# One GIN graph layer on one core: register loads of 32, copies moved to VectorE, 22 gathered rows a group on both queues, a reordered end

## What is computed

```
h   = relu(layernorm(x))
agg = segment_sum(h[src], dst)            # 200000 rows gathered
t   = relu(batchnorm(((1 + eps) h + agg) @ W1 + b1))     # 512 wide
y   = t @ W2 + b2 + h
out = x + relu(batchnorm(y))
```

## Time and profile before

| | |
|---|---|
| median of 3 runs | 3151.29 us (3143.07 to 3159.94) |
| the profiled execution | 3149.71 us |
| its span (first to last instruction) | 3147.9 us |
| around the span | 1.8 us |
| granted TensorE clock, mean | 0.72 |
| busy: PE / PEld / DVE / ACT / POOL | 46 / 29 / 20 / 15 / 45 % |

### The profile page before, as it was taken

The page is one execution under the profiler, slowest core; times in us unless marked ns, Lnnn a source line. Parts: engine busy times, 40 slices in busy tenths (PEclk is TensorE's granted clock), DMA queues, the critical chain, the costliest instruction groups (busy, mean ns, idle before and its releaser), DMA issues.

```text
span 3147.9 us, 31339 instructions
## 1 busy us (share of the span) xinstructions
PE 1454.9 (46%) x4883; PEld 918.7 (29%) x4883; DVE 632.1 (20%) x1628; ACT 472.7 (15%) x979; POOL 1431.3 (45%) x1518
## 2 busy tenths in 40 slices
PE   2443444444434434443352453344444253444999
PEld 2222222333222222232231232222223132322546
DVE  6454531111101101111011011011011010111346
ACT  4553530000000000000000000000000000000445
POOL 5645455555444453454344544544544454553000
PEclk7766677776776776776676766767766666767999
DMA  5544432332222222222222322222322222233646
GB/s 162 169 142 145 135 111 87 93 100 79 86 87 71 87 87 78 85 87 80 75 73 84 96 71 80 83 82 87 93 74 80 76 90 80 79 92 120 235 161 255
DMA packets 129207, 325.72 MB, mean 103 GB/s; under 512 B 35641, under 2 KB 61594, under 8 KB 122862
## 3 DMA queue, kind: packets, MB, share of 16 engines
q0 software_dynamic: 72384, 197.75, 21.3%
q1 hardware_dynamic: 43946, 99.32, 8.8%
q10 hardware_dynamic: 12676, 26.68, 2.6%
HBM read 271.56 MB, written 52.05 MB: 103 GB/s over the span
## 4 chain that ended last, share of the span: by engine, by line
SPq 47%; issue 28%; PE 8%; ACTq 2%; another core or an unknown queue 0%; DVE 0%; ACT 0%; DVEq 0%; DMA 0%
SPq L482 38%; SPq L477 8%; PE ps L1345 5%; ACTq L1102 2%; PE ps L1359 1%; SPq L446 1%; PE ps L1301 0%; PE ps L1228 0%; PE ps L1263 0%; SPq L467 0%; SPq L451 0%; ACTq L1098 0%; DVE aggT L789 0%; DVE st L632 0%
## 5 line engine op out<-in xcount | busy, mean ns | idle before, releaser
L606 POOL DMA_INDIRECT arena<-h_rows,arena x1272 | 1205.4, 948 | 1262.9 <-PE ps L1228 755.7
L1228 PE MATMUL ps<-arena 128*96 128x256 f32 x3016 | 940.1, 478 | 754.1 <-issue 217.9
L1228 PEld LDWEIGHTS ps<-arena 128*96 128x96 f32 x3016 | 624.2, 212 | 1047.0 <-issue 619.9
L1254 PE MATMUL ps<-ident,arena 128*128 128x128 f32 x196 | 55.6, 381 | 668.7 <-ACT aggT L1055 357.5
L606 POOL DMA_INDIRECT arena<-in_x,arena x220 | 208.5, 948 | 197.2 <-PE ps L1228 112.6
L828 DVE BATCH_NORM_STATS2 arena<-arena 128x6 f32<-128x512 f32 x92 | 63.7, 693 | 1080.4 <-ACT arena L1071 788.9
L1254 PEld LDWEIGHTS ps<-ident,arena 128*128 128x128 f32 x196 | 26.8, 183 | 717.9 <-issue 685.3
L789 DVE TENSOR_TENSOR aggT<-aggT,ps 128x192 f32 x196 | 69.4, 354 | 739.6 <-PE ps L1238 357.4
L1263 PE MATMUL ps<-arena 128*128 128x512 f32 (+3 forms) x412 | 209.9, 639 | 1.3 <-DVE arena L820 1.1
L1062 ACT COPY arena<-ps 96x256 f32<-96x256 f32 x196 | 71.8, 367 | 899.1 <-issue 688.6
L1055 ACT COPY aggT<-ps 128x256 f32<-128x256 f32 x98 | 36.0, 369 | 1039.6 <-issue 1025.6
(11 more groups left out here) (94 smaller groups left out, 532.8 us busy)
## 6 DMA issues: line engine op xcount, KB each, us to landing
rl_odd<-h_rows SPq DMA_DIRECT2D x3456, 1.0 KB
W2s<-h_rows ACTq DMA_DIRECT2D x3072, 1.0 KB
t_T<-arena SPq DMA_DIRECT2D x24, 1024.0 KB, 3.8
arena<-t_T SPq DMA_DIRECT2D x24, 1024.0 KB, 4.8
arena<-h_rows,arena POOLq DMA_INDIRECT x1272
arena<-in_x SPq DMA_DIRECT2D x27, 512.0 KB, 5.6
h_rows<-arena ACTq DMA_DIRECT2D x24, 512.0 KB
out<-arena SPq DMA_DIRECT2D x23, 512.0 KB
```

What stands on the lines that cost most here:

```text
L606: nc.gpsimd.indirect_dma_start(out=rows[slot(g)][:, k, :], out_offset=None, in_=(x if g < H_FROM else h_dram)[:, :], in_offset=bass.Indire ...
L1228: last = T.matmul(win_ps[g % 2], sel[:, g % 2, k, :], rows_of(g, k), start=k == 0, stop=k == n - 1)
L1254: last = T.transpose(hT[:, f, 0:n], h[0:n, f * P:(f + 1) * P], ident[0:n, 0:n])
```

## The change

Seven edits:

1. SP and ScalarE load 32 row addresses at a time instead of 16 (AT_ONCE); each register is freed once its row is issued.
2. ScalarE's share rises from 20 to 22 rows a group (ACT_EIGHTHS = 11). It then fetches 27 tiles instead of 24, and GpSimd 1505 instead of 1508. SP's share stays at 22 rows a group, counted in eighths.
3. From group 31 (COPIES_FROM) on the copies `keep_window`, `keep_hT` and `t_and_b1` of the main loop are VectorE's. The last ones, after the loop, stay ScalarE's.
4. Inverse, shift and normalisation of group 0 stand ahead of the flag.
5. SP stores the last full chunk of t after its wait for all windows, not before it.
6. y is added, measured and signalled for each half f by itself, on TensorE and on VectorE; the residual addition and the store of the last output chunk are cut into two halves.
7. `keep_warm` around the last groups: 8, 3, 10 and 26 multiplications become 4, 1, 6 and 12.

```diff
-SP_QUARTERS = 11
-ACT_QUARTERS = 5
+SP_EIGHTHS = 22
+ACT_EIGHTHS = 11
+COPIES_FROM = H_FROM + 1
+AT_ONCE = 32
...
             def load_rows(j, m):
...
-                regs = [sp.alloc_register(f"row{j}_{m}_{k}") for k in range(PIECE)]
-                sp.reg_load(regs, sp_at[j % 2][0:1, m * PIECE:(m + 1) * PIECE])
+                if m * PIECE % AT_ONCE == 0:
+                    regs = [sp.alloc_register(f"row{j}_{m}_{k}") for k in range(AT_ONCE)]
+                    sp.reg_load(regs, sp_at[j % 2][0:1, m * PIECE:m * PIECE + AT_ONCE])
+                    row_regs.extend(regs)
                 for k in range(PIECE):
                     e = m * PIECE + k
-                    at = sp.snap(regs[k], donate=True, min_val=0, max_val=(N - 1) * ROW_BYTES)
+                    reg = row_regs.pop(0)
+                    at = sp.snap(reg, donate=True, min_val=0, max_val=(N - 1) * ROW_BYTES)
...
-                for reg in regs:
                     sp.free_register(reg)
...
+            sp.wait_ge(s_add, NG)
             store_t(NQF - 1)
-            sp.wait_ge(s_add, NG)
             for q in range(X_FIRST):
                 load_x(q)
...
             statistics(0)
             mean_and_var(0)
+            inverse(0)
+            shift(0)
...
+            def keep_hT(c):
+                n = rows_of_node_tile(c)
+                dve.wait_ge(s_zt, c + 1)
+                dve.wait_ge(s_hTc, c)
+                hT = hT_ps if c < NT - 1 else hT_last
+                V.tensor_copy(aggT[:, :, c * P:c * P + n], hT[:, :, 0:n]).then_inc(s_hTc, 1)
+
+            def keep_window(w):
+                dve.wait_ge(s_agg, w + 1)
+                dve.wait_ge(s_ev, w)
+                dve.wait_ge(s_wT, w - 1)
+                V.tensor_copy(win_sb[w % 2], win_ps[w % 2]).then_inc(s_ev, 1)
+
+            def t_and_b1(q, m):
+                dve.wait_ge(s_t, FB * q + m + 1)
...
+                V.tensor_scalar(tb[:, m, :], t_ps[(FB * q + m) % TB][:, 0:QN], b1T[:, m:m + 1], None, ALU.add
+                                ).then_inc(s_tb, 1)
...
+                if g >= COPIES_FROM:
+                    keep_window(g - 2)
...
+                if g >= COPIES_FROM and m < FB:
+                    t_and_b1(q, m)
                 selection(g)
                 if g % 2 == 1 and g >= 7:
                     z_tile((g - 7) // 2)
+                    if g >= COPIES_FROM:
+                        keep_hT((g - 7) // 2)
...
                 for f in range(DB):
+                    dve.wait_ge(s_c, DB * q + f + 1)
                     y = aggT[:, f, q * QN:q * QN + n]
...
-            keep_warm(26, 1)
+            keep_warm(12, 1)
...
-                last.then_inc(s_c, 1)
+                    last.then_inc(s_c, 1)
```

More of the change, by code:

```diff
@@ L94, in build, with eighths @@
         H_ACT = H_FROM - 1
-        def quarters(q, n):
-            return q * n // 4
+        def eighths(q, n):
+            return q * n // 8
         per_tile = P // PIECE
@@ L101, in build @@
         while True:
-            done = ceil(4 * per_tile * (len(sp_groups) + 1), SP_QUARTERS)
+            done = ceil(8 * per_tile * (len(sp_groups) + 1), SP_EIGHTHS)
             if done > H_NODES or 2 * (done - 1) + 6 >= H_FROM:
@@ L107, in build @@
         while True:
-            done = ceil(4 * per_tile * (len(sp_groups) - SP_X + 1), SP_QUARTERS) + H_NODES
+            done = ceil(8 * per_tile * (len(sp_groups) - SP_X + 1), SP_EIGHTHS) + H_NODES
             if 2 * (done - 1) + 6 >= NG - 4:
@@ L114, in build @@
         while True:
-            done = ceil(4 * per_tile * (len(act_groups) + 1), ACT_QUARTERS) + H_ACT
+            done = ceil(8 * per_tile * (len(act_groups) + 1), ACT_EIGHTHS) + H_ACT
             if done - 1 + 4 >= NG - 4:
@@ L200, in build @@
         W1s = piece[1].rearrange("p (k n) -> p k n", n=F)
+        assert COPIES_FROM % 2 == 1 and COPIES_FROM > max(H_ACT, 2 * H_NODES + 2, NQ + 2)
         W2s = sb("W2s", [P, FB, D])
@@ L492, in pieces_of_pass @@
                 if c < H_NODES:
-                    return row_pieces(quarters(SP_QUARTERS, c), quarters(SP_QUARTERS, c + 1), SP_X)
+                    return row_pieces(eighths(SP_EIGHTHS, c), eighths(SP_EIGHTHS, c + 1), SP_X)
                 c -= H_NODES
-                return [(SP_X + j, m) for j, m in row_pieces(quarters(SP_QUARTERS, c), quarters(SP_QUARTERS, c + 1),
+                return [(SP_X + j, m) for j, m in row_pieces(eighths(SP_EIGHTHS, c), eighths(SP_EIGHTHS, c + 1),
                                                             len(sp_groups) - SP_X)]
@@ L555, in _ @@
                                  (in_0, in_1, s_u, FB * (last[0] + 1)),
-                                 (at_u + 2, in_0, s_c, last[1] + 1),
-                                 (at_u, at_u + 2, s_c, last[0] + 1)):
+                                 (at_u + 2, in_0, s_c, DB * (last[1] + 1)),
+                                 (at_u, at_u + 2, s_c, DB * (last[0] + 1))):
                 for i in range(m, end):
@@ L569, in store_out @@
                                  x_place(i)[a:b, :, :]).then_inc(s_o, 16)
-            for i in range(NQ):
+            for i in range(NQ - 1):
                 store_out(i)
-            sp.wait_ge(s_o, 16 * sum(len(row_parts(last_order(i)[1])) for i in range(NQ)))
+            q, n = last_order(NQ - 1)
+            for b in (0, 1):
+                sp.wait_ge(s_sum, NQ + b)
+                sp.dma_start(out[q * QN:q * QN + 4 * n, :].rearrange("(p b k) d -> p b (k d)", b=2, k=2)[:, b, :],
+                             x_place(NQ - 1)[:, b, :]).then_inc(s_o, 16)
+            sp.wait_ge(s_o, 16 * (2 + sum(len(row_parts(last_order(i)[1])) for i in range(NQ - 1))))
         @block.gpsimd
@@ L946, in y_chunk @@
                 n = QN if q < NQF else TAILN
-                dve.wait_ge(s_c, q + 1)
                 for f in range(DB):
+                    dve.wait_ge(s_c, DB * q + f + 1)
                     y = aggT[:, f, q * QN:q * QN + n]
[L950 to L953, removed]
+                    V.scalar_tensor_tensor(y, c_ps[q % 2][f][:, 0:n], b2T[:, f:f + 1], y, ALU.add, ALU.add
+                                           ).then_inc(s_y, 1)
+                    dve.wait_ge(s_y, DB * q + f + 1)
                     at = 3 + 6 * (q - AHEAD2)
@@ L971, in residual @@
                 dve.wait_ge(s_oT, i + 1)
-                V.tensor_tensor(x_place(i, n), o_ps[i % 2][0:n, :, :], x_place(i, n), ALU.add).then_inc(s_sum, 1)
+                if i < NQ - 1:
+                    V.tensor_tensor(x_place(i, n), o_ps[i % 2][0:n, :, :], x_place(i, n), ALU.add).then_inc(s_sum, 1)
+                else:
+                    for b in (0, 1):
+                        z = x_place(i, n)[:, b, :]
+                        V.tensor_tensor(z, o_ps[i % 2][0:n, b, :], z, ALU.add).then_inc(s_sum, 1)
             for i in range(NQ):
@@ L1121, in step @@
                 if g >= H_ACT:
-                    for j, m in row_pieces(quarters(ACT_QUARTERS, g - H_ACT), quarters(ACT_QUARTERS, g - H_ACT + 1),
+                    for j, m in row_pieces(eighths(ACT_EIGHTHS, g - H_ACT), eighths(ACT_EIGHTHS, g - H_ACT + 1),
                                            len(act_groups)):
@@ L1134, in step @@
                 q, m = divmod(g - 2 * PG * Q + 1, PG * Q)
-                if q >= 0 and m < FB:
+                if q >= 0 and m < FB and g < COPIES_FROM:
                     t_and_b1(q, m)
@@ L1143, in _ @@
             a, c, q = NG - 4, NT - 4, NQF - 2
+            act.wait_ge(s_ev, a - 2)
+            act.wait_ge(s_hTc, c - 1)
+            act.wait_ge(s_tb, FB * q + 1)
             keep_window(a - 2)
-            keep_hT(c - 2)
             t_and_b1(q, 1)
```

40 lines of the change are left out of this document (25 added, 15 removed).

## The result

The changed kernel is slower, by 0.8%. Its median is 3172.39 us over 17 runs against 3151.03 us of the kernel before in the same sets; the ratio is 1.0076, 95% interval 1.0049 to 1.0103. The profiled execution has a span of 3170.5 us, 22.6 us more than before. The forecast was 3122 us, the range ended at 3168: the time lies outside it, on the side of the slower rivals.

A forecast was written before the change was run, and what follows sets the result against it. The prediction took SP's list to bound the h phase. Its terms were -13 (h phase), -7 (group 0 early), -3 (x-phase loads) and -5 us (end): 3149.7 - 28 = 3122 us, range 3060 to 3168, 8 in 10.

The forecast's parts named there:

- the slower rivals: Queues holding each other up in bursts (3181 us, chance 0.17); load costing per register (3159 us, chance 0.18).
- What bounds it: h phase, 2435 of 3148 us: lasts as long as SP's list takes, slower while GpSimd runs 16 gathers (a burst).
- the model: One pass of h, two groups, 44 SP rows: 30.84 us, 78.5 passes; 1.116 us a row in bursts, 0.419 outside.
- The step that failed: Bursts: ScalarE's 22 rows and freed queue raise SP's own row from 1.024 to 1.065 us, the pass to 30.68.
- the second rival: Bursts: queues hold each other up, SP's row 1.20 us instead of 1.024; 3181 us, chance 0.17.
- the 688.6 us row of its idle time: Profile row on ScalarE: idle time ended by issue, its copies often starting only when its queue reached them.
- The loads of 32: SP's address loads: 1.95 us each, half as many; 33 us saved in h with all else as it is.
- The third rival: Address loads: cost per register, 2.36 us for 32, so nothing saved on loads; 3159 us, chance 0.18.
- Copies on VectorE: h phase: some 150 us more work on VectorE, 290 busy of 2435; TensorE's `keep_hT` wait goes, costed at nothing.
- the cover that the prediction named: h phase: SP's rows are late next, so the copies' move shows no gain unless SP stops being the bound.
- Start: Before h: group 0's aggregate at about 48 us, SP's list 7 us earlier; loads of 32 in x phase, -3 us.
- End: After h: shorter warming -3.7 us, y by halves -0.8, last store in halves -0.5; together -5.

The follow-up runs named there:

- c32_sp20: The changed kernel with ScalarE at 20 rows a group, copies on ScalarE and SP at 20 rows a group: 0.9393 of the kernel before, 3001.8 us.
- c32_sp18: As c32, with SP's share at 18 rows a group instead of 22: 0.8891 of the kernel before, median 2825 us.
- c32_again: c32 again in the third set: start, end and loads of 32, with ScalarE's 20 rows and copies as before; 0.9868 of the kernel before.
- after_again: The changed kernel itself, measured again in the third set: 1.0073 of the kernel before.
- a_act20: The changed kernel with ScalarE at 20 rows a group again, everything else as changed: 0.9978 of the kernel before, 3138 us.
- a_copies_act: The changed kernel with all copies on ScalarE again, everything else as changed: 0.9998 of the kernel before, 3144 us.
- d_waits: The changed kernel at 20 ScalarE rows, copies on VectorE, ScalarE waiting where its copies stood: 0.9957 of the kernel before, repeated 0.9955, both without slow steps.
- act20_again: The changed kernel at 20 rows a group on ScalarE, without added waits, in a set without slow steps: 1.0040 of the kernel before.
- c32_third: c32 in the fifth set, without slow steps: start, end and loads of 32 alone; 0.9952 of the kernel before.
- b_fill: The kernel before with eight tiny unread writes more on VectorE in each group from 31 on: 1.0048 of the kernel before.
- a_at16: The changed kernel with 16 addresses a load again on both queues, everything else as changed: 1.0175 of the kernel before, 3195 us.
- a_ends: The changed kernel with loads of 16, 20 ScalarE rows and copies on ScalarE, leaving only start and end edits: 0.9984 of the kernel before, 3143 us.
- c32: The changed kernel with ScalarE at 20 rows a group and the copies on ScalarE: 0.9822 of the kernel before, second set.
- a_act8: The changed kernel with ScalarE at 8 rows a group, 9 tiles instead of 27, GpSimd 1523: 0.9695 of the kernel before.

## Why the prediction was wrong

**What bounds it** was right where the steps are slow: SP's list. The experiments with 20 and 18 rows show it (c32_sp20, c32_sp18), with a gain near the one that the model gives. One reading was off and cost nothing: the wait of 9.7 us comes after SP's last row, not among its rows.

**The step that failed** is the row's own price inside a burst: "I take 1.065, near the lower end: ScalarE already issued through most of each burst, and only its waits are filled." The distance between SP's rows in a run of gathers rose from 1.169 to 1.268 us, by 0.099, although a row carries 0.010 less of loads. So the row itself went from 1.024 to about 1.13 in the model's terms (estimate; the distance is a rough measure, but the 107 rows pushed out of the runs give the same 33 us). With that and a load of 2.06 us the pass becomes 31.19 us, +0.35 x 78.5 = +27 us; measured were +33, forecast -13. The premise was mis-sized too: ScalarE stood still for 521 us of the phase before, and for 171 after. I had the 688.6 us row of its idle time in hand and did not turn it into SP's price.

It is the second rival in a milder form (1.13 instead of 1.20, 3172 instead of 3181 us). That ScalarE's edits are the loss is shown: undone together they give 2% in one set (c32_again against after_again). There are two causes of like size, worth some 31 and 25 us when undone: the 384 rows more (a_act20) and the copies' move (a_copies_act). How the second works is shown only where the gathers don't slow the queues: there it sets ScalarE's queue free (d_waits against act20_again and c32_third). Where they do, and where the prediction was made, d_waits has not run, and b_fill speaks for a share of VectorE's own instructions; so there the mechanism is argued. Whether SP is slowed by the other queue's instructions or by the DMAs that they start was not separated either.

**The loads of 32.** Price 2.06 us on SP and 2.24 on ScalarE; 1.95 was taken, and the straight line through VectorE's 0.304 gave 2.12. The saving was forecast at 33 us with all else as it is. Undoing them cost about 1.0% or 31 us (a_at16 against the changed kernel, give or take 0.5 points); the model gives 24 us for 2.06. The third rival, no gain per register, is out: two loads of 16 cost 2.36 us, one of 32 costs 2.06. The Trainium skill's 200 ns a register ("Runtime: NRT & Kernel Launch", "Instruction fetch mechanics") is three times the 64 ns measured here. The page speaks of the runtime's own register loads, from HBM; those here read SBUF, so the two are not prices of the same thing.

**Copies on VectorE cost nothing by themselves.** Right in the h phase without slow steps (d_waits), wrong as an account: what they released was priced as a small thing. And the cover that the prediction named, SP's rows being late, ends with SP's last row. From there to the first product with W2 it is 54.3, 55.1, 55.2 and 56.8 us with the copies on ScalarE and the new end (a_ends, c32, c32_again, a_copies_act), and 58.1 to 60.0 with them on VectorE (changed, a_act20, a_at16, a_act8, after_again).

**Start.** Forecast -7 and -3; the first row of h came 9.7 us earlier. Group 0's aggregate started at 50.2, not at 48. That the first row of h agrees so well is partly luck: with the same start it came at 440 to 463 us elsewhere.

**End.** Forecast -3.7 up to the first product with W2; measured -3.6 over the stretch where the warm multiplications stood, with the clock at 1.00 in it and behind it. The lower clock of the last groups (0.89 against 0.96) is not the shorter warming's: it is 0.50 from 2915 to 2921 us, behind 6.5 us in which TensorE stood idle, and the first shortened warm multiplications come at 2948.39. Forecast -1.3 for y and the last store, measured -1.6. Not foreseen: +4.4 between SP's last row and those last windows, where VectorE stands 31.5 us before a block of t with the selection behind it.

## What to carry to other kernels

When one engine's in-order list is the bound, price every edit of another queue by what it does to that list: a queue that is freed of its waits issues more in the same time, and here that cost more than the work it took over. Taking work off the bound itself was worth far more than the rest: 4 rows fewer a pass gave 4 to 5%, by one constant, where the loads of 32 gave about 1%. And before sharing work out more evenly, see which list is late; here a share that raised the second queue to the level of the first made the first later. Where no steps were slow, GpSimd bounded the kernel with ScalarE's queue held, and taking rows off SP's list gained nothing.

## What was not expected of the hardware

- The same kernel took 3147 to 3196 us in three sets and 2126 to 2130 us in two. In the first three sets single steps of the queues take 0.70 us while GpSimd's gathers run, and SP's and ScalarE's lists both show it; in the last two GpSimd gathers with hardly a pause (1.25 us each) and SP's 48 rows take 18.04 us (c32_third) where they took 33.19 before. The five sets ran on chips with the numbers 1, 14, 0, 1 and 14, so each number that came twice was once slow and once fast. Whether the same number is the same chip is not known, and so it is open whether the speed belongs to a chip or to the moment; nothing in the traces names the cause.
- Also in the last two sets ScalarE's row issues slow SP's: 0.42 us a row with ScalarE held, 0.45 with it free (without SP's waits), though outside GpSimd's runs in the first set no such effect showed (0.41 us in all kernels).
- A register load costs 0.30 to 0.48 us for one, 1.18 for 16, 2.06 for 32 on SP: 55 ns for each of the second sixteen.
- 1300 tiny writes on VectorE, which is not the bound, moved the time by 0.5% (0.2 to 0.8).
